# Moving two squares and some scans within a hand-written order: a fused two-layer decoder on one core

## What is computed

```python
x = layernorm(x + random_features(x))           # 1
x = layernorm(x + attention16(x, ctx, ctx))     # 2
x = layernorm(x + coupling_rotations(x))        # 3: three cycles of a four-layer network, then a rotation
x = layernorm(x + state_space(x))               # 4: four chunks of 128 channels, 16 states each
x = layernorm(x + gated(x, ctx, ctx, ctx))      # 5
x = layernorm(x + experts(x))                   # 6: eight experts, top one kept
```

## Time and profile before

| | |
|---|---|
| median of 3 runs | 3413.72 us (3413.61 to 3415.29) |
| the profiled execution | 3415.3 us |
| its span, first to last instruction | 3413.5 us |
| mean granted clock of TensorE | 0.827 |
| busy: PE, DVE, ACT, POOL | 76%, 74%, 50%, 44% |

### The profile page before, as it was taken

One profiled execution on the slowest core, in us unless ns is written; L12 is line 12 of the kernel. 1 busy time (PEld: TensorE's weight loads), 2 busy tenths in 40 slices (PEclk: granted clock), 3 DMA queues, 4 the chain that ended last, 5 costly groups with the idle time before them and its releaser, 6 DMA issues.

```text
span 3413.5 us, 41544 instructions
## 1 busy us (share of the span) xinstructions
PE 2603.7 (76%) x10956; PEld 1509.9 (44%) x10956; DVE 2515.0 (74%) x4320; ACT 1722.0 (50%) x3078; POOL 1492.6 (44%) x1159
## 2 busy tenths in 40 slices
PE   4985787868778786877878688687877878787556
PEld 2544444444445443444444344444444445444323
DVE  2258678696877869687786968778696886859683
ACT  1456454546546464564646455454655545456430
POOL 1036354463525446253543625355362544526370
PEclk8767798888888888888888889888887988869677
DMA  3000000000000000000000000000000000000000
GB/s 118 10 7 9 13 10 13 15 13 6 9 19 9 13 12 3 19 9 19 9 13 12 3 19 9 13 15 13 12 3 19 9 13 6 7 6 0 12 5 8
DMA packets 16849, 45.72 MB, mean 13 GB/s; under 512 B 2248, under 2 KB 7056, under 8 KB 16400
## 3 DMA queue, kind: packets, MB, share of 16 engines
q1 hardware_dynamic: 16656, 43.96, 3.8%
HBM read 35.57 MB, written 8.39 MB: 13 GB/s over the span
## 4 chain that ended last, share of the span: by engine, by line
PE 47%; DVE 24%; issue 13%; ACT 12%; DVEq 1%; POOL 1%; ACTq 0%; DMA 0%; SPq 0%; POOLq 0%
PE bank L522 45%; DVE h_ring L1065 10%; ACT a_ring L1447 6%; DVE x L1163 2%; DVE smax L969 2%; PE bank L404 1%; ACT spare L1347 1%; DVE qT L1019 1%; DVE couple L1016 1%; DVE x12T L1021 1%; POOL ysum L1635 1%; DVE soft L1044 1%; DVE ln_stats L378 1%; DVE x L396 1%; ACT L1453 1%
## 5 line engine op out<-in xcount | busy, mean ns | idle before, releaser
L1635 POOL TENSOR_TENSOR ysum<-ysum,h_ring 128x512 f32<-128x512 f32 x896 | 1150.3, 1284 | 723.0 <-DVE h_ring L1065 660.3
L1065 DVE TENSOR_TENSOR_SCAN h_ring<-a_ring,bank 128x512 f32<-128x512 f32 x1024 | 1170.0, 1198 | 53.6 <-POOL ysum L1635 43.3
L522 PE MATMUL bank<-w_expert_w,x45T 128*128 128x512 f32 x1024 | 578.3, 712 | 228.1 <-DVE x L1163 226.6
L1447 ACT ACTIVATE a_ring<-soft,decay 128x510 f32<-128x510 f32 x1024 | 651.3, 707 | 25.7 <-DVE h_ring L1065 24.0
L522 PEld LDWEIGHTS bank<-w_expert_w,x45T 128*128 128x128 f32 x1024 | 223.8, 227 | 534.2 <-DVE x L1163 288.4
L1622 POOL TENSOR_TENSOR soft<-xc,soft 128x512 f32<-128x512 f32 x64 | 82.1, 1294 | 748.7 <-ACT soft L1418 748.7
L522 PE MATMUL bank<-x3T,w_winT 128*128 128x512 f32 x512 | 276.3, 673 | 22.5 <-ACT x3T L410 13.1
L522 PE MATMUL bank<-spare,w_cn_w 128*128 128x256 f32 x768 | 235.2, 444 | 74.5 <-ACT spare L1377 64.5
L1163 DVE SCALAR_TENSOR_TENSOR x<-bank,weight,x 128x256 f32<-128x256 f32 x512 | 213.3, 472 | 65.7 <-PE bank L522 65.7
L522 PE MATMUL bank<-qT,kmask 32*120 32x256 f32 x1024 | 215.3, 513 | 57.4 <-ACT spare L1347 56.8
L969 DVE TENSOR_REDUCE smax<-bank 128x4 f32<-128x480 f32 x256 | 156.2, 651 | 118.7 <-PE bank L522 118.7
(11 more groups left out here) (145 smaller groups left out, 4069.2 us busy)
## 6 DMA issues: line engine op xcount, KB each, us to landing
x0T<-in_xT SPq DMA_DIRECT2D x16, 512.0 KB, 3.2
x<-in_x SPq DMA_DIRECT2D x16, 512.0 KB, 3.4
out<-x SPq DMA_DIRECT2D x16, 512.0 KB, 2.8
ctxT<-in_ctxT SPq DMA_DIRECT2D x16, 240.0 KB, 2.5
ctxTb<-in_ctxT SPq DMA_DIRECT2D x16, 240.0 KB, 2.6
ctxb<-in_ctx SPq DMA_DIRECT2D x16, 240.0 KB, 3.0
w_expert_w<-in_expert_w SPq DMA_DIRECT2D x1, 2048.0 KB
w_winT<-in_winT SPq DMA_DIRECT2D x1, 1024.0 KB
```

Source lines behind the costliest of these rows:

```text
L522: return pe.matmul(o, l, r, start=start, stop=stop)
L1065: scanned.then(v.tensor_tensor_scan(h_ring[:, k % HRING, :], a_ring[:, k % RING, :, :].rearrange("p b s -> p (b s)"), xc2, 0.0, ALU.mult, ...
L1447: a.activation(a_ring[:, k % RING, :, 1:S], delta[:, c, :].rearrange("p (b s) -> p b s", b=NB)[:, :, 1:S], ACT.Exp, scale=decay[:, k:k + 1 ...
L1635: p.tensor_tensor(out=total, in0=first, in1=h_ring[:, k % HRING, :], op=ALU.add)\
```

## The change

Two of the four squares are moved on ACT: that of chunk 2 from ahead of decay 34 to ahead of decay 43, that of chunk 3 from ahead of decay 48 to ahead of decay 59. On DVE, three scans (27 to 29) are moved up between the second rotation and the expert sums `combine(b, 4, 6)`, one plan step more (scan 32) is run ahead of `values` and `combine(b, 6, 8)`, three scans (42 to 44) are moved up between the fourth rotation and `combine(b, 8, 10)`, and scan 48 is moved ahead of `combine(b, 10, 12)`. No instruction is added or removed; PE, POOL and the DMA queue keep their order.

```diff
-SQUARE_AT = (0, 20, 34, 48)
+SQUARE_AT = (0, 20, 43, 59)
...
                     rotate(f, 0)
                     rotate(f, 1)
+                states(m, 31)
                 if b is not None:
                     combine(b, 4, 6)
-                states(m, 33)
+                states(m, 34)
                 if nxt is not None:
                     values(nxt)
...
                     rotate(f, 2)
                     rotate(f, 3)
+                states(m, 47)
                 if b is not None:
                     combine(b, 8, 10)
-                states(m, 50)
+                states(m, 51)
                 if b is not None:
                     combine(b, 10, 12)
                 states(m, 52)
```

## The result

The changed kernel is slower: 3454.93 us as the median of four runs (3454.49 to 3455.66), against 3414.05 for the kernel before, timed beside it. The ratio is 1.0119 [1.0102, 1.0137]. The forecast was 3386. The profiled execution took 3455.66 us, for a span of 3453.9.

The account below looks back on a forecast made before the run. With no engine full, the bound was sought inside a turn, in DVE's waits (1.57, 1.23, 2.44 us). 13 x 1.8 = 23.4 plus 2.5, 0 and 1.5 gave 27.4 off 3413.7: 3386 us, range 3374 to 3398 (65%).

Parts of the forecast that it names:

- Scans into the expert wait: DVE behind the second rotation: scans 27 to 29 fill the waits for experts 4 and 5, costing 0.27 us.
- The square of chunk 2: Between scans 31 and 32: bare square costs 0.75 us, of it 0.67 idle; DVE 2.3 ahead after sums 6 and 7.
- The gate: Third rotation's gate: second cycle starts earlier on ACT, gate at 1507.5, so DVE's 2.44 us wait mostly goes.
- The third and fourth rotation: Starts under POOL's sums, two of ten operations slowed to end with POOL's last two; rotations end 3.0 us ahead.
- Rival 2: POOL's sums don't hinder the third rotation: 3.3 us ahead a pass, 3367 us; chance 8%.
- rival 3: POOL loses too beside the rotation, one more operation (1.33 us) in the way: 0.5 ahead a pass, 3403 us; 11%.
- Three scans ahead of sums 8 and 9: Scans 42 to 44 start the sums 0.36 us later; PE idles some 7 ahead of expert 10, `ln1_sum` waits 0.4.
- Rival 1: PE starved by the three scans ahead of sums 8 and 9: `ln1_sum`'s second half 1.2 us later, 3429 us; 8%.
- the 1.8 of the forecast: At the second half of the `ln1_sum` addition, DVE is ahead by 1.8 us, with all scans up to 49 done.
- The rest of the pass: Behind `ln1_sum`, order unchanged: DVE had no wait, everything follows DVE, so 1.8 us a pass is carried through.
- The sum: Whole kernel: 13 x 1.8 = 23.4 us in the loop, with the other turns 27.4 off 3413.7, giving 3386 us.
- the 4.0 forecast for the turns outside the loop: Gains outside the 13 passes: turn 1 2.5 us, turn 15 0, turn 16 1.5.

Follow-up runs that it names:

- added products: Six unread 128x512 products on PE ahead of `gated_out`: 3478.17 us in the changed kernel, 3403.22 in the kernel before, 3363.53 in the smaller change.
- smaller change: Against the kernel before: squares at 43 and 59, three scans ahead of sums 4 and 5, other scans as before; 3372.32 us, again 3384.68.
- delay of seven: Changed kernel with seven unread batch-norm statistics on DVE ahead of the turn's last three scans; 3414.12 us.
- delay of four: Changed kernel with four unread batch-norm statistics on DVE ahead of the turn's last three scans; 3446.07 us.
- less work: Kernel before, its own order, with the last four scans of a group run over half of the positions; 3488.4 us.
- order alone: Kernel before with only DVE's order changed, the squares where they were; 3467.2 us.
- two statistics in the kernel before: Kernel before with two added unread batch-norm statistics on DVE, 0.65 us a turn; 3461.14 us.

## Why the prediction was wrong

By its own steps:

- *Scans into the expert wait.* Right: no wait ahead of the four sums.
- *The square of chunk 2*, and that of chunk 3. Each idle is 0.86, not the 0.67 of the earlier trace rows: two terms mis-sized by 0.2. ACT had nothing else in hand, as said.
- *The gate.* Right in effect: no wait ahead of the third rotation.
- *The third and fourth rotation.* Right: the operations that begin under POOL's sums took 1.26 and 1.44, and two of ten did. Rival 2 (no hindrance) falls. The same timeline on POOL:

```profile
1526.58 6.65 POOL L1637 TENSOR_TENSOR ysum<-ysum,h_ring 128x512 f32<-128x512 f32 x5 [0.17 <-DVE h_ring L1065]
```

  POOL's five sums took 6.65 beside the rotation, 6.64 before it: POOL loses nothing, rival 3 falls. A lock that makes whichever comes second wait, as the Trainium skill has it (SBUF — State Buffer, "SBUF: two separate sides"), shows here on DVE's side only.
- *Three scans ahead of sums 8 and 9.* Right in kind. PE on experts 10 and 11, then on `first_project`, in the changed kernel:

```profile
1541.12 5.41 PE L522 MATMUL bank<-w_expert_w,x45T 128*128 128x512 f32 x8 [9.01 <-DVE x L1163]
1546.37 3.62 PE L522 MATMUL bank<-w_rfwT,feats 128*128 128x256 f32 x16
```

  PE idled 9.01 ahead of them (7 forecast), the two experts took 5.41 (5.6), and `ln1_sum` didn't wait (0.4). Rival 1 is refuted: the slower kernel isn't slower by it. From the last operation of the second rotation to `ln1_sum` it was 43.57 us before (1484.26 to 1527.83) and is 41.77 now (1507.72 to 1549.49): the 1.8 of the forecast came, 1.80. That it is so exact is luck, as two idles that were put 0.2 too short and a wait of 0.4 that didn't come cancel.
- ***The rest of the pass*, "Transposes, norms and the next turn follow DVE. So I carry 1.8 through": this failed.** "DVE had no wait there" was read from rows that end near 1553; behind them DVE waits for PE. An addition there, first in the kernel before, then in the changed one:

```profile
1570.90 0.69 DVE L371 TENSOR_TENSOR x<-bank,x 128x512 f32<-128x512 f32 x1 [1.21 <-PE bank L522]
1591.72 0.69 DVE L371 TENSOR_TENSOR x<-bank,x 128x512 f32<-128x512 f32 x1 [0.45 <-PE bank L522]
```

  Up to here the 1.8 was carried; here some 0.8 came on top, and with 0.6 lost ahead of the second rotation the changed part came to 2.06. Then the next turn's attention, taken as a fixed length because nothing of it was touched and it follows DVE, went from 59.86 to 65.33: it follows PE, and PE's clock in it fell from 0.77 to 0.63.
- *The sum.* Without that step it would have held for the loop: 13 x 2.06 = 26.8 won, against 23.4 said. Less 13 x 5.47 = 71.1, it is 44.3 lost there. That the 3.9 left over is near the 4.0 forecast for the turns outside the loop is chance: the attentions of turns 1, 2 and 15 alone moved by 4 to 9 us, up and down.

What was overlooked stood in the profile: the pass had been read at one clock, and PE's clock was weighed only behind PE's idle ahead of expert 10. No rival had the clock of the attention, 0.77 before, as a quantity that could change.

One sign can be read off the clock's records in the profiles: where in the pass, counted from the square of chunk 0, the clock first falls. The first 7 us are alike in every pass compared (PE busy for 5.93 to 5.95 us, clock 1.00, in seven of the runs), and yet that fall comes anywhere from 7.3 to 9.0 us. In turns 2 to 15 of the eleven profiles without added products (154 attentions), all 60 with the fall at 7.9 to 8.3 us took 59.6 to 59.9 us. The 32 with an earlier fall, up to 7.7, took 63.0 to 68.8; the 55 with a later one, from 8.35 on, 60.4 to 66.7; the seven at 7.73 to 7.76 took either 59.7 or 68.7. So the same work meets the clock at different points, and a shift of half a microsecond in that decides over several.

What stays open: why the clock came back in the third window of 6 us in one kernel and not in the other, after work that differed by less than 1 us in time, and so which shifts are good. The runs show that it depends on more than the order and the work, and that a delay or a shortening of 2 us or less is enough to turn it; they don't give a rule by which to place a pass.

## What to carry to other kernels

In a loop with idle time on PE, compare stage by stage, with the granted clock beside each length, also the stages that a change leaves alone: a gain of 2 us in one may cost 5 in the next. Give a forecast for such a kernel a case in which the clock of an untouched stage changes, priced from its rows at either level. And don't judge an order by one timing: try neighbours of it, with a small delay or one move fewer, before it is thrown away or kept.

## What was not expected of the hardware

Passes of most versions settle on few lengths, whatever was moved: 197.97 (smaller change), 201.39 (before, and the change with a delay of seven), 204.80 (the change, and with a delay of four), 208.2 (less work, order alone). Neighbours are 3.4 us apart. Three versions don't settle but alternate between lengths, also others than these, as 201.5 to 201.8 and 211.1 with two statistics in the kernel before. So a small gain or loss in a stretch doesn't show in the pass as it is: mostly the attention takes up the difference, and the changed part too (two statistics, 0.65 us by the estimate, made it 1.5 to 2.1 longer). Why just these lengths wasn't tried.

PE can be busy without a break and stay at the lower level: for 13.63 us at the end of the changed kernel's attention, for 33.36 us in the change with the added products.
